# Group statistics one round earlier, and a factor from a tensor, in a pipelined window-attention kernel

## Time and profile before

| | kernel before |
|---|---|
| three executions | 948.2, 947.55, 951.34 us |
| profiled execution | 949.39 us |
| its span | 947.6 us |
| mean granted TensorE clock | 0.946 of full speed |
| TensorE matmul busy | 756.3 us |
| GpSimd busy | 552.4 us |
| ScalarE busy | 517.6 us |
| VectorE busy | 509.7 us |

### The profile page before, as it was taken

The page is one execution under the profiler, slowest core; times in us unless marked ns, Lnnn a source line. Parts: engine busy times, 40 slices in busy tenths (PEclk is TensorE's granted clock), DMA queues, the critical chain, the costliest instruction groups (busy, mean ns, idle before and its releaser), DMA issues.

```text
span 947.6 us, 38578 instructions
## 1 busy us (share of the span) xinstructions
PE 756.3 (80%) x15518; PEld 658.4 (69%) x15518; DVE 509.7 (54%) x1177; ACT 517.6 (55%) x848; POOL 552.4 (58%) x913
## 2 busy tenths in 40 slices
PE   4588787887887788788798787887788788888985
PEld 3576676776776676677676676776676677777874
DVE  3455564465465564564655565465564565465542
ACT  3455555565565555564555555565555565565641
POOL 2466556556556656656656556556656656556652
PEclk9789999899899999998989999899999999999995
DMA  5652000000000000000000000000000000000010
GB/s 127 166 166 80 1 1 0 0 0 0 0 0 0 0 0 0 0 0 0 1 0 0 22 22 11 22 22 11 22 22 11 22 22 11 22 22 11 22 37 26
DMA packets 14041, 21.45 MB, mean 23 GB/s; under 512 B 3756, under 2 KB 5045, under 8 KB 14005
## 3 DMA queue, kind: packets, MB, share of 16 engines
q1 hardware_dynamic: 13461, 20.23, 7.1%
q10 hardware_dynamic: 544, 0.79, 0.2%
HBM read 12.60 MB, written 8.42 MB: 22 GB/s over the span
## 4 chain that ended last, share of the span: by engine, by line
POOL 42%; issue 34%; PE 10%; DMA 4%; DVE 4%; POOLq 2%; SPq 2%; ACT 1%; DVEq 0%
POOL probs L971 26%; PE ps_qk L380 4%; DMA x_all<-in_x 4%; POOL xn L927 4%; POOL refined L955 2%; POOL refined L953 2%; POOL refined L951 2%; POOL root L961 2%; POOL mean_sq L935 2%; POOL bn L938 1%; PE ps_mix L500 1%; POOL bn L936 1%; POOL g_off L964 1%; PE ps_score L427 1%; PE ps_score L420 1%
## 5 line engine op out<-in xcount | busy, mean ns | idle before, releaser
L380 PE MATMUL ps_qk<-w_qk,xn 128*128 128x512 f32 x768 | 226.6, 451 | 138.7 <-POOL xn L927 136.6
L971 POOL TENSOR_TENSOR probs<-probs,exp_bias 128x512 f32<-128x512 f32 x256 | 321.0, 1286 | 15.0 <-ACT probs L647 15.0
L380 PEld LDWEIGHTS ps_qk<-w_qk,xn 128*128 128x128 f32 x768 | 160.8, 216 | 187.2 <-issue 145.6
L761 DVE TENSOR_REDUCE sums_sq<-squares 128x32 f32<-128x512 f32 x128 | 87.3, 682 | 314.0 <-ACT squares L578 314.0
L578 ACT ACTIVATE squares<-ps_qk 128x512 f32<-128x512 f32 x128 | 76.6, 598 | 218.9 <-PE ps_qk L380 218.9
L647 ACT ACTIVATE probs<-ps_score,lower 128x1024 f32<-128x1024 f32 x128 | 142.3, 1113 | 40.9 <-PE ps_score L480 40.9
L500 PE MATMUL ps_mix<-v_ones,probs 64*64 64x17 f32 x8192 | 133.9, 209 | 0.5 <-issue 0.5
L500 PEld LDWEIGHTS ps_mix<-v_ones,probs 64*64 64x64 f32 x8192 | 127.5, 136 | 9.4 <-issue 1.0
L935 POOL TENSOR_TENSOR mean_sq<-bn 128x4 f32<-128x4 f32 x64 | 16.5, 257 | 187.7 <-DVE bn L753 187.7
L512 PE MATMUL ps_qk<-w_v,xn 128*128 128x256 f32 x768 | 109.4, 292 | 5.6 <-DVE unit L786 4.6
L512 PEld LDWEIGHTS ps_qk<-w_v,xn 128*128 128x128 f32 x768 | 96.1, 191 | 16.6 <-issue 16.4
(11 more groups left out here) (71 smaller groups left out, 893.6 us busy)
## 6 DMA issues: line engine op xcount, KB each, us to landing
x_all<-in_x SPq DMA_DIRECT2D x32, 256.0 KB, 2.9
out<-x_out SPq DMA_DIRECT2D x32, 256.0 KB, 2.1
bias_rev<-table_scratch SPq DMA_DIRECT2D x4, 452.0 KB
w_qk_in<-in_L_matrices ACTq DMA_DIRECT2D x1, 512.0 KB, 4.6
w_o_in<-in_L_matrices SPq DMA_DIRECT2D x4, 128.0 KB
w_qk_in<-in_L_matrices SPq DMA_DIRECT2D x1, 512.0 KB, 3.9
w_v_in<-in_L_matrices ACTq DMA_DIRECT2D x1, 256.0 KB, 5.0
w_v_in<-in_L_matrices SPq DMA_DIRECT2D x1, 256.0 KB, 5.1
```

The lines of the kernel that those rows point to most:

```text
L380: last = nc.tensor.matmul(ps_qk[:, e, :], xn[:, px, t.parity, c, e * P:(e + 1) * P], w_qk[:, pw, c, :], start=(c == 0 and i == 0), stop=(c ...
L761: nc.vector.tensor_reduce(sums_sq[:, e * NORMS:(e + 1) * NORMS], squares[:, e, :].rearrange("p (h d) -> p h d", d=HD), AX_X, ALU.add).then ...
L971: nc.gpsimd.tensor_tensor(pr, pr, exp_bias[:, t.layer, r, :, :, :, :].rearrange("p e c a n -> p (e c a n)"), ALU.mult).then_inc(weighted, 1)
```

## The change

`moments(ahead)` is called at the head of VectorE's round, ahead of the first norm sum, and no longer behind `divide`; rounds with j below 0 keep their order. The last operation of the group variance, max and then times 4, becomes a scalar_tensor_tensor whose factor comes from a tensor `fours` in SBUF that GpSimd fills at the start, in place of an immediate. The number of memsets counted goes from 5 to 6, and VectorE waits for them once, ahead of the first group variance.

```diff
+        fours = sb("fours", [P, CC])
...
-        FILLS = 5
+        FILLS = 6
...
                 past(dve, gn_offset, u.count(1, 0))
+                if j == 1 - WARM and not base.exact:
+                    dve.wait_ge(filled, FILLS)
...
-                nc.vector.tensor_scalar(sums_sq[:, 2 * NORMS:], g_var[:, :], EPS_GN, 4.0, ALU.max, ALU.mult).then_inc(gn_step, 1)
+                nc.vector.scalar_tensor_tensor(out=sums_sq[:, 2 * NORMS:], in0=g_var[:, :], scalar=EPS_GN, in1=fours[:, :], op0=ALU.max, op1=ALU.mult).then_inc(gn_step, 1)
...
+                if j >= 0:
+                    moments(ahead)
                 sum_norms(base, now, 0)
...
                 divide(older)
-                if j >= 0:
-                    moments(ahead)
                 refine_shift(before)
...
+            nc.gpsimd.memset(fours[:, :], 4.0).then_inc(filled, 1)
             nc.gpsimd.memset(threes[:, :], 3.0).then_inc(filled, 1)
```

## The result

The changed kernel took **794.26 us** (median of 4 runs, 792.12 to 796.29), the kernel before 948.67 us in the same comparison (4 runs, 947.55 to 951.34): ratio 0.8369, 95% interval 0.8339 to 0.8398. The forecast was 789 us, with 778 to 802 as the likeliest case's own range and 733 to 822 as the whole. The profiled execution took 793.52 us with a span of 791.6 us.

What follows compares the result with a forecast made beforehand. It took a cycle of waits to bound the kernel: bn_stats, split of xn, projection. Round 2's start 41.28, 59 x 11.52 = 679.7, 1.5 and 66.2 gave a span of 788.7, against the median 789.3; range 733 to 822 us.

Steps and rivals of the forecast that it cites:

- likeliest case: Whole kernel: the move removes the stall before the projection, the new form gains nothing; 789 us, chance 0.68.
- The bound: Looped round: GpSimd waits 187.7 us for bn_stats, then TensorE's q/k projection waits 136.6 us for the split of xn.
- The move: bn_stats at the head of VectorE's round: 2.39 us go from TensorE's stop before the projection, 13.89 becomes 11.50.
- cover of the split: GpSimd's split of xn, 0.99 us later behind the mean squares, still ends 1.1 us ahead of the projection.
- The new form: Variance's last operation on VectorE, two SBUF inputs: still waits for GpSimd's multiplication in flight, 0 gained.
- The first rival: The new form does not wait, or slips between two multiplications: rounds of 10.7 us, 741 us; chance 0.18.
- The period: Loop left through L812's wait, multiplications to scores to next multiplications: 11.48 and 11.57, mean 11.52 us a round.
- The late GpSimd: Rival: bn_stats beside GpSimd's work make its multiplications end up to 0.8 us later; 12.3 a round, 835 us; chance 0.10.
- The clock: TensorE's projections without idle time in front keep full clock, twelve matmuls in 2.97 and 2.96 us; no slow round counted.
- half-clock rival: TensorE, without its pauses, is held at 1.2 GHz: rounds of 16 us, 1054 us; chance 0.02.
- 59 x 11.52: Term for rounds 2 to 60 at the new period: 679.7 us.
- the 1.5 us added for the rounds between the layers: Estimated addition for rounds that split weights and mask the bias between the layers, most of it hidden: 1.5 us.

Runs made afterwards that it cites:

- Experiment 4: Kernel before, with GpSimd's split of xn queued ahead of its mean squares and VectorE's order untouched: 791.9 us, ratio 0.8357.
- experiments 1 and 2: Each against the kernel before: 1, statistics moved, variance's last operation in its old form, 793.74 us; 2, new form alone, statistics unmoved, 949.65 us.
- Experiment 3: Changed kernel with the variance g_var in PSUM instead of SBUF, so the last operation has one SBUF and one PSUM input: 742.37 us, ratio 0.7824.
- experiment 5: Changed kernel with each first-layer image load waiting on SyncE for the projections of the round before: 792.78 us, ratio 0.8352.

## Why the prediction was right, and where the 5 us are

**The bound.** That a wait of GpSimd for bn_stats, handed on through the split of xn to the projection, set the round: right. Experiment 4 broke that chain at another link, and the wait on TensorE went with it; that its time is so nearly the same is the coincidence told there.

**The move.** Predicted to take all of TensorE's stop before the projection; it did. The mean squares were expected 8.1 us into the round and began at 319.27 - 310.86 = 8.41; bn_stats were expected at 10.7 and began at 10.76. The cover of the split was thinner than the forecast's 1.1 us ahead of the projection, 322.32 - 321.55 = 0.77, and held.

**The new form.** Predicted to gain nothing against the old; experiments 1 and 2 show it on both sides. The first rival needed 0.16 us from it and rounds of 10.7 us. Experiment 3 shows that the price put on that rival was right as well: where the operation does not wait, the round is 10.6 us and the kernel 742.37 us, against 741 in the rival's sum. What failed was only its condition, and by the rival's own clock: L815 started at 3.69 us into the round, the fourth multiplication at 310.64 - 310.86 + 3 x 1.257 = 3.55. The forecast had 3.79 and 3.56, so the margin of 0.23 us shrank to 0.14 and held; an operation that starts over 0.14 us sooner would have met the third multiplication.

**The period.** The loop of multiplications, L815, mixed, scores and exponential was worked out as 11.48 and 11.57. In the changed kernel its two parts are 319.67 - 315.67 = 4.00 and 327.15 - 319.67 = 7.48 (327.15 is 322.11 + 5.04): 11.48. Rounds alternate 11.46 and 11.57.

**The late GpSimd.** The divide now runs beside the split: the reciprocal at 320.50 lies wholly within it and takes 0.35 us, with hardly any spread (352 to 354 ns). bn_stats meet GpSimd less than the rival assumed. In the round shown they start at 321.62, after the split's end at 321.55, and only the second of them overlaps the multiplications, by 322.37 - 322.11 = 0.26 us. They take 410 ns each at the median, and four multiplications take 5.03 and 5.04 us, before 5.01 to 5.03. So the rival fell: neither is longer where the two overlap. But only 10 of the 128 bn_stats lie beside GpSimd over nearly their whole length (407 ns at the median), so it is tested on short overlaps in the main.

**The clock.** Over the 54 rounds from 103.55 to 725.32 us the granted clock was 1.00, in the kernel before 0.96 from 103 to 881 us; twelve matmuls of the projection took 2.96 us. Rounds without those pauses weren't slowed, and the half-clock rival fell. One early round was slow, though the forecast counted none (below).

**Where it was off.** The forecast was 5 us low, and the term that was mis-sized is 59 x 11.52 for rounds 2 to 60. Round 2 began at 41.15 (forecast 41.28), and from the projection of round 61, at 725.32, to the end it is 66.3 us (forecast 66.2). Between them lie 684.2 us, and the forecast had 679.7 + 1.5 = 681.2. Projections of the opening rounds:

```profile
41.15 3.06 PE L381 MATMUL ps_qk<-w_qk,xn 128*128 128x512 f32 x12
...
54.43 2.95 PE L381 MATMUL ps_qk<-w_qk,xn 128*128 128x512 f32 x12
...
66.88 2.95 PE L381 MATMUL ps_qk<-w_qk,xn 128*128 128x512 f32 x12
...
79.58 2.98 PE L381 MATMUL ps_qk<-w_qk,xn 128*128 128x512 f32 x12
...
92.40 2.95 PE L381 MATMUL ps_qk<-w_qk,xn 128*128 128x512 f32 x12
```

Rounds 2 to 5 took 13.28, 12.45, 12.70 and 12.82 us, together 51.25 against 4 x 11.52 = 46.08, so 5.2 too long; round 6, to the projection at 103.55, took 11.15 and gave 0.4 back. Rounds 3, 4 and 5 hold the stalls of experiment 5, 3.2 us in sum. Round 2 holds none; there the granted clock was 0.58 from 46 to 54 us, after a wait of 1.55 us for the probabilities, and the mix took 3.24 us in place of 2.06. The 54 rounds from 103.55 to 725.32 took 621.8 us, 54 x 11.52 = 622.1, so that the 1.5 us added for the rounds between the layers weren't needed. 5.2 - 0.4 - 0.3 - 1.5 = 3.0, the span's miss. The other 2 us are the spread of single executions: the profiled one of the kernel before lay 1.2 us above its median, that of the changed kernel 0.7 below its own.

The kernel before had such stalls too, amid its scores and value projections (56.04, 71.71, 85.24 and 99.51 us, 0.56 to 0.99 each). The forecast took its rounds from 570 us on and let them stand for the opening as well; the trace's first rounds would have shown the stalls.

## What to carry to other kernels

An engine's queue hands a wait on to everything behind it: when a wait is long, look at what stands behind it and who waits for that, and then move either the work that comes late or the work that is stuck. A round that the trace happens to show without the wait, here the last rounds with no image three ahead, can price the change: it gave 11.50 us here, and 11.46 and 11.57 were measured. And a tiny instruction with a median six times its minimum is a wait in disguise: ask where its inputs lie before changing what it computes.

## What the runs showed of the hardware

An operation of VectorE on two elements waited for GpSimd's 1.25 us multiplication in flight when it read two tensors from SBUF (1132 ns at the median) and also as tensor_scalar with one tensor and an immediate (1141 ns); with one of two inputs in PSUM it took 159 ns at the same place, which was worth 52 us (794.26 to 742.37). Reciprocal and tensor_reduce, each with one SBUF input, ran beside GpSimd at the 0.35 and 0.69 us that they take alone; bn_stats overlapped GpSimd only in part, by some 0.2 us, and kept their 0.41 us.

TensorE stood still 0.7 to 1.6 us three times in the first rounds of every kernel here, 249 and 250 matmuls apart, at the same instructions whether or not loads ran beside it; what it waits for there is open.
